# A gated cross-attention and expert layer: the row of score maxima is split by row group, and the next batch's queries move from units 0 to 3 to units 4 to 7

## What is computed

```python
# x (16,100,128), ctx (16,1444,96)
q = ln(x) @ w_q;  k = ctx @ w_k;  v = ctx @ w_v            # 16 heads of 64
attn = softmax(q @ k.T / 8)                                # 100 x 1444 per head
x = x + tanh(g_xattn) * ((attn @ v) @ w_o + b_o)
x = x + tanh(g_ffn) * ffn(ln(x))    # self-attention, 16 heads of 8, then top 2 of 8 experts + shared
```

## Time and profile before

| what | us |
|---|---|
| median of 3 runs (range) | 1325.35 (1325.32 to 1327.8) |
| the profiled execution's own time | 1323.73 |
| its span, first to last instruction | 1322.0 |
| TensorE busy | 1249.3 (95%) |
| VectorE busy | 935.8 (71%) |
| ScalarE busy | 824.1 (62%) |
| GpSimd busy | 767.5 (58%) |
| granted TensorE clock, mean | 0.984 of full speed |

### The profile page before, as it was taken

How to read it: one execution, slowest core, us unless ns; L and a number is a source line. 1 busy time by engine, 2 the same in 40 slices (tenths; PEclk the granted TensorE clock), 3 DMA queues, 4 the chain that set the end, 5 groups by cost and what they waited for, 6 DMA issues and landing times.

```text
span 1322.0 us, 34615 instructions
## 1 busy us (share of the span) xinstructions
PE 1249.3 (95%) x14472; PEld 911.7 (69%) x14472; DVE 935.8 (71%) x1714; ACT 824.1 (62%) x1476; POOL 767.5 (58%) x603
## 2 busy tenths in 40 slices
PE   6789999999999999999999999999999999789998
PEld 5356777777677777777776767677777776567776
DVE  5697776768675868685858676767767685956676
ACT  1345666667666766666666666666666666555654
POOL 3144666565656566665656565756565646654554
PEclk9798999999999999999999999999999999999999
DMA  6201503030313030302020302111021300000000
GB/s 172 65 1 34 167 14 80 14 80 14 81 13 81 13 80 14 80 10 77 13 74 15 78 16 55 40 41 53 18 75 14 63 14 15 14 15 1 8 8 14
DMA packets 122278, 57.28 MB, mean 43 GB/s; under 512 B 108262, under 2 KB 117706, under 8 KB 122122
## 3 DMA queue, kind: packets, MB, share of 16 engines
q1 hardware_dynamic: 122122, 55.07, 17.5%
HBM read 15.38 MB, written 0.82 MB: 12 GB/s over the span
## 4 chain that ended last, share of the span: by engine, by line
PE 73%; DVE 13%; ACT 10%; issue 3%; DMA 1%; SPq 0%; DVEq 0%; ACTq 0%
PE psum L777 17%; PE psum L758 9%; PE psum L858 8%; PE psum L759 8%; PE psum L760 8%; PE psum L793 5%; PE psum L890 3%; PE psum L912 3%; PE psum L903 3%; PE psum L805 3%; DVE mx L1309 3%; DVE p_lo L449 2%; DVE kbd L1329 2%; ACT p L985 2%; ACT p_hi L991 2%
## 5 line engine op out<-in xcount | busy, mean ns | idle before, releaser
L449 POOL TENSOR_TENSOR p_lo<-p,p_hi 128x768 f16<-128x768 f32 (+1 forms) x192 | 349.6, 1827 | 256.0 <-ACT p_hi L986 163.3
L1309 DVE TENSOR_REDUCE mx<-psum 128x1 f32<-128x512 f32 (+1 forms) x585 | 360.8, 651 | 38.5 <-PE psum L858 32.9
L985 ACT ACTIVATE p<-psum 128x768 f32<-128x768 f32 (+1 forms) x256 | 215.0, 840 | 243.6 <-PE psum L760 243.4
L777 PEld LDWEIGHTS psum<-c_both,p_hi 128*128 128x128 f16 x4992 | 255.2, 98 | 61.7 <-issue 30.3
L777 PE MATMUL psum<-c_both,p_hi 128*128 128x97 f16 (+1 forms) x4992 | 281.2, 207 | 2.1 <-ACT acc_sb L1001 1.1
L758 PE MATMUL psum<-qk_hi,cT_both 97*128 97x384 f16 (+1 forms) x768 | 259.6, 338 | 17.2 <-ACT p_hi L991 9.1
L759 PE MATMUL psum<-qk_lo,cT_both 96*128 96x384 f16 (+1 forms) x768 | 258.4, 336 | 0.0
L760 PE MATMUL psum<-qk_hi,cT_both 96*128 96x384 f16 (+1 forms) x768 | 256.3, 334 | 0.0
L858 PE MATMUL psum<-cT_both,qk_hi 96*128 96x512 f16 (+1 forms) x585 | 215.9, 369 | 10.9 <-DVE kbd L1329 4.9
L449 DVE TENSOR_TENSOR p_lo<-p,p_hi 128x768 f16<-128x768 f32 (+1 forms) x192 | 205.0, 1068 | 16.7 <-ACT p_hi L986 15.3
L990 ACT ACTIVATE p<-psum 128x384 f32<-128x384 f32 (+1 forms) x256 | 130.0, 508 | 135.5 <-PE psum L760 135.5
(11 more groups left out here) (201 smaller groups left out, 2115.7 us busy)
## 6 DMA issues: line engine op xcount, KB each, us to landing
c_both<-c_new SPq DMA_DIRECT2D x16, 768.0 KB, 3.5
ctx_nat<-in_ctx_dram SPq DMA_DIRECT2D x16, 528.0 KB
aT<-a_new SPq DMA_TRANSPOSE x64, 2.9
wg<-in_L_ffn_e_gate_dram SPq DMA_DIRECT2D x1, 1024.0 KB, 5.5
wu<-in_L_ffn_e_up_dram SPq DMA_DIRECT2D x1, 1024.0 KB, 7.8
wd<-in_L_ffn_e_down_dram SPq DMA_DIRECT2D x8, 128.0 KB, 4.9
out_dram<-x SPq DMA_DIRECT2D x4, 200.0 KB
x<-in_x_dram SPq DMA_DIRECT2D x1, 600.0 KB
```

Of the source, the lines that this page charges most:

```text
L449: engine.tensor_tensor(p_lo[0:m, i % 3, 0:w], p32[0:m, i % 3, 0:w], p_hi[0:m, i % 3, 0:w], ALU.subtract).then_inc(lo_made(b, i)[0], 1)
L777: t = mm(psum[:, ACCB + bank, k * (C + 1):k * (C + 1) + wide], p[0:m, i % 3, n * P:(n + 1) * P], c[parity][0:m, j, 0:wide], start=(j == 0 ...
L985: a(to32, src, ACT.Exp, scale=DH ** -0.5)
L1309: v.tensor_reduce(mx[:, rt, part:part + 1], bank[:, 0:w], AX.X, ALU.max)\
```

## The change

The maxima are split by row group. Those of the first (tiles 0 to 5, 18 of the 39) and of two more tiles (`AHEAD`, 24) are still found a batch ahead, now in units 10 to 23 of the batch before; the other 15 (tiles 8 to 12) are found as units "o" in units 0 to 9 of the batch itself. Each group gets its own transposition (m in unit 21, m1 in unit 10), its own `mrow` and its own DMAs: `send_second_row` sends tiles 6 to 11 and the short tile 12, and unit 12 (`i == CH`) waits for them. The next batch's queries are made in units 4 to 7. Ahead of batch 0 only 8 tiles are reduced, and m stands behind the sixth. In batch 0 the layer-norm units move to units 0 to 10, and ScalarE's conversion of batch 1's context goes from unit 0 to unit 3. The last batch now has the 15 o units and m1. The diff, cut to its core:

```diff
-    for n, i in enumerate((0, 1, 2, 3)):
+    for n, i in enumerate((4, 5, 6, 7)):
         plan[i].append(("q", n))
...
-    share = {i: 0 for i in range(3, 21)}
-    for n in range(NPU):
-        i = min(share, key=lambda i: (load[i], i))
...
+    NP0 = TILES[0] * MP
+    AHEAD = NP0 + 2 * MP
...
+    for i, n in spread(range(AHEAD, NPU), range(10)):
+        plan[i].append(("o", n))
+    for i, n in spread(range(NP0), range(10, 21)) + spread(range(NP0, AHEAD), range(21, UNITS)):
+        plan[i].append(("p", n))
+    plan[10].append(("m1", 0))
+    plan[21].insert(0, ("m", 0))
...
+    LN_UNITS = ((0, 1, 3, 4), (3, 4, 6, 7), (6, 7, 9, 10))
+    RSTD_UNITS = (2, 5, 8)
     for n in range(1, 4):
-        plan[2 * n + 5].append(("la", n))
-        plan[2 * n + 6].append(("lb", n))
-        plan[2 * n + 8].append(("lc", n))
-        plan[2 * n + 9].append(("x", n))
+        for kind, i in zip(("la", "lb", "lc", "x"), LN_UNITS[n - 1]):
+            plan[i].append((kind, n))
...
-    PREP = [("q", 0), ("q", 1)] + [("w", n) for n in range(3)] + [("q", 2)] + \
-           [("w", n) for n in range(3, 6)] + [("q", 3)] + [("w", n) for n in range(6, RT)] + [("m", 0)]
+    PREP = [("q", 0), ("q", 1)] + [("w", n) for n in range(3)] + [("q", 2)] + [("w", n) for n in range(3, 6)] + \
+           [("m", 0), ("q", 3)] + [("w", n) for n in range(6, AHEAD // MP)]
...
-        mrow = sb("mrow", [RT, P], F16)
+        mrow = [sb(f"mrow{r}", [TILES[r], P], F16) for r in range(2)]
...
             def send_row(b, parity, free):
 
                 sp.wait_ge(aux_free, free + 1)
-                sp.dma_start(qk_hi[parity][C:C + 1, 0:(RT - 1) * P], mrow[0:RT - 1, :]).then_inc(row_in, 16)
+                sp.dma_start(qk_hi[parity][C:C + 1, 0:ROW0[1]], mrow[0][:, :]).then_inc(row_in, 16)
+
+            def send_second_row(b, parity, free):
+
+                sp.wait_ge(aux_free, free + 1)
+                sp.dma_start(qk_hi[parity][C:C + 1, ROW0[1]:(RT - 1) * P], mrow[1][0:TILES[1] - 1, :]).then_inc(row2_in, 16)
                 sp.dma_start(qk_hi[parity][C:C + 1, (RT - 1) * P:ROWS],
-                             mrow[RT - 1:RT, 0:rows_of(RT - 1)]).then_inc(row_in, 16)
+                             mrow[1][TILES[1] - 1:TILES[1], 0:rows_of(RT - 1)]).then_inc(row2_in, 16)
...
                     ctx_made(b + 1, 1 - parity)
                     turn(b - 1, 1)
+                    second_row_of(b, kind, parity)
...
                 if i == 0:
-                    pe.wait_ge(row_in, (b + 1) * 32)
+                    pe.wait_ge(row_in, (b + 1) * 16)
+                    if isinstance(b, int) and b == 0:
+                        pe.wait_ge(wide_free, AHEAD // MP)
+                if i == CH:
+                    pe.wait_ge(row2_in, (b + 1) * 32)
...
-                    if kind == "first" and i == 0:
+                    if kind == "first" and i == 3:
                         ctx_hi_parts(1, kind, 1)
...
-                    if n == NPU - 1:
+                    if n in (NP0 - 1, NPU - 1):
+                        r = int(n == NPU - 1)
+                        tiles = (slice(0, TILES[0]), slice(TILES[0], RT))[r]
                         dve.wait_ge(aux_free, free + 1)
-                        v.tensor_reduce(mx_row[:, :], mx[:, :, :], AX.X, ALU.max).then_inc(max_step, 1)
+                        v.tensor_reduce(mx_row[:, tiles], mx[:, tiles, :], AX.X, ALU.max).then_inc(max_step, 1)
...
-                    cp(mrow[:, :], bank[0:RT, 0:P // 2].bitcast(F16)).then_inc(aux_free, 1)
+                    cp(mrow[r][:, :], bank[0:TILES[r], 0:P // 2].bitcast(F16)).then_inc(aux_free, 1)
```

More of the change, by code:

```diff
@@ L85, in flamingo_kernel, with spread @@
         load[i] += 0 if i - 1 in LO_POOL else .9
-    share = {i: 0 for i in range(3, 21)}
-    for n in range(NPU):
-        i = min(share, key=lambda i: (load[i], i))
[L89 to L96, removed]
+    NP0 = TILES[0] * MP
+    AHEAD = NP0 + 2 * MP
+    def spread(maxima, units):
+        counts = {i: 0 for i in units}
+        for _ in maxima:
+            i = min(counts, key=lambda i: (load[i], i))
+            counts[i] += 1
+            load[i] += .6
+        left = iter(maxima)
+        return [(i, next(left)) for i in units for _ in range(counts[i])]
+    for i, n in spread(range(AHEAD, NPU), range(10)):
[4 more added lines that the diff above has]
+    plan[21].insert(0, ("m", 0))
     ROUTER = ["max", "sub", "sum", "inv", "prob", "best0", "tie0", "rank0", "first0", "pick0", "drop",
@@ L160, in one_maxima_first @@
     def one_maxima_first(units):
-        maxima = [u for u in units if u[0] == "p"]
+        maxima = [u for u in units if u[0] in ("p", "o")]
         if sum(u[0] not in NO_BANK for u in units) < 3 or not maxima:
@@ L169, in places_of @@
         banked = [u for u in units if u[0] not in NO_BANK]
-        early = bool(banked) and banked[0][0] == "p"
+        early = bool(banked) and banked[0][0] in ("p", "o")
         where = {0: [], 1: [3], 2: [1, 3], 3: [0, 1, 3] if early else [1, 2, 3], 4: [0, 1, 2, 3] if early else [1, 1, 2, 3],
@@ L210, in flamingo_kernel @@
     LN_A, LN_B = ["sum", "mean", "centred"], ["square", "sumsq", "lnvar"]
+    SET_NAMES = {"la": lambda n: [f"{k}{n}" for k in LN_A], "lb": lambda n: [f"{k}{n}" for k in LN_B],
+                 "lc": lambda n: [f"xln{n}"], "x": lambda n: [f"xhi{n}"], "nh": lambda n: [f"Nh{n}"],
+                 "x1": lambda n: [f"x1 {n}"]}
     SET_DVE = [f"{n}0" for n in LN_A + LN_B] + ["wqT", "xln0", "Mh0hi", "Mh0", "xhi0", "xlnT0", "tn", "bot", "Mh1lo"] + \
-              [f"{n}1" for n in LN_A + LN_B] + [f"{n}2" for n in LN_A] + ["xln1"] + [f"{n}2" for n in LN_B] + \
-              ["Nh0", "xhi1"] + [f"{n}3" for n in LN_A] + ["Nh1", "xln2"] + [f"{n}3" for n in LN_B] + \
-              ["Nh2", "xhi2", "x1 0", "Nh3", "xln3", "x1 1", "xhi3", "x1 2", "x1 3"]
+              [name for us in steps("first")[0] for place in us for k, n in place if k in SET_NAMES
+               for name in SET_NAMES[k](n)]
     SET_ACT = ["wkT", "tx", "tf", "Mh1", "wvT"]
@@ L528, in row_of, with second_row_of @@
                 send_row(b + 1, 1 - parity, aux_base(b, kind)[1] + steps(kind)[1][("m", 0)][1])
+            def second_row_of(b, kind, parity):
+                if kind != "first":
+                    sp.wait_ge(scores, b * UNITS)
+                send_second_row(b, parity, aux_base(b, kind)[1] + steps(kind)[1][("m1", 0)][1])
             ctx_made(0, 0)
+            send_row(0, 0, numbered(PREP)[("m", 0)][1])
             ctx_made(1, 1)
-            send_row(0, 0, AT_FIRST - 1)
+            second_row_of(0, "first", 0)
             turn(0, 0)
@@ L551, in _ @@
             turn(B - 2, 1)
+            second_row_of(B - 1, "last", 1)
             turn(B - 1, 0)
@@ L673, in body @@
                 for i in range(UNITS):
-                    if kind == "first" and i in (9, 11, 13):
-                        token_rstd((i - 7) // 2)
+                    if kind == "first" and i in RSTD_UNITS:
+                        token_rstd(RSTD_UNITS.index(i) + 1)
                     if i == CTX_LO_AT and b + 2 < B:
@@ L854, in aux @@
                         pe.wait_ge(ct_in, (b + 1) * 16)
-                    if part == 0 and rt % 3 == 0 and rt // 3 < 4:
+                    if kind == "p" and part == 0 and rt % 3 == 0:
                         pe.wait_ge(aux_free, out_of(("q", rt // 3)))
@@ L859, in aux @@
                            cT_hi[parity][0:C, part * MW:part * MW + w], start=True, stop=True)
-                elif kind == "m":
-                    pe.wait_ge(max_step, (b + 1) * 2)
-                    t = tr(bank[0:RT, 0:P // 2].bitcast(F16), mneg[:, :], ident16[:, :])
+                elif kind in ("m", "m1"):
+                    r = int(kind == "m1")
+                    tiles = (slice(0, TILES[0]), slice(TILES[0], RT))[r]
+                    pe.wait_ge(max_step, (2 * b + r + 1) * 2)
+                    t = tr(bank[0:TILES[r], 0:P // 2].bitcast(F16), mneg[:, tiles], ident16[:, :])
                 elif kind == "x":
@@ L1283, in aux @@
                     scores_of = psum[:, 3 * (n % 2):3 * (n % 2) + MP, :].rearrange("p b w -> p (b w)")[:, 0:KV]
-                    v.tensor_reduce(mx_row[:, n:n + 1], scores_of, AX.X, ALU.max).then_inc(wide_free, 1)
-                    if n == RT - 1:
-                        dve.wait_ge(wide_free, RT)
-                        ts(mneg[:, :], mx_row[:, :], -1.0, SHIFT, ALU.mult, ALU.add).then_inc(max_step, 2)
+                    if n == TILES[0]:
+                        set_wait(dve, set_pool, SET_POOL, "mx")
+                    into = mx_row[:, n:n + 1] if n < TILES[0] else mx[:, n, 0:1]
+                    v.tensor_reduce(into, scores_of, AX.X, ALU.max).then_inc(wide_free, 1)
+                    if n == TILES[0] - 1:
+                        dve.wait_ge(wide_free, TILES[0])
+                        ts(mneg[:, 0:TILES[0]], mx_row[:, 0:TILES[0]], -1.0, SHIFT, ALU.mult, ALU.add).then_inc(max_step, 2)
                     return
```

31 lines of the change are left out of this document (18 added, 13 removed).

## The result

The changed kernel takes 1404.98 us (median of 4 runs, 1403.3 to 1406.28), the kernel before 1325.34 beside it (4 runs, 1323.58 to 1327.8). The ratio is 1.0606, with a 95% interval of 1.0591 to 1.0622: 6% slower, where I had forecast half a per cent faster. The profiled span is 1403.8 us instead of 1322.0.

What follows compares the result with a forecast made beforehand. TensorE, busy for 95% of the span, was taken as the bound. Stretch ahead -9.4, batch 0 -4, middle batches +4.2 and last batch +3 sum to -6.2: 1325.35 - 6.2 = 1319 us, range 1305 to 1333.

Steps and rivals of the forecast that it cites:

- (a): Middle batch, units 4 to 7: queries ahead of probs_rest and a maximum on VectorE make TensorE wait; +1.25 us a batch.
- the ring of banks: Middle batch: three banks go round, so o37 waits 1.0 us for o35's bank, and q1 in unit 5 0.25 for q0's.
- the one on the slow side: The second row makes it slower: TensorE waits 1.8 us at unit 12, time 1335 us; chance 0.26.
- The rest of the middle batch: Middle batch: costs 1.25, 0.8 and 0.1 less gains of 1.85 give +0.3 us, times fourteen +4.2.
- The gains: Middle batch: of 2.3 us lost, 0.45 stays (0.2 in units 1 to 3, 0.25 in 22 and 23); -1.85 us.
- Unit 5: Middle batch, unit 5: its earlier loss of 0.4 us goes, and q1 waiting for q0's bank costs 0.25.
- (b): Unit 12: the second row, copied behind kbd and three reductions, lands late; TensorE waits 0.8 us in each batch.
- the estimate beside it: Unit 12: a fixed DMA cost of about 2.0 us from the Trainium skill makes the row's wait 1.1 us.
- The stretch ahead: Ahead of batch 0: five of thirteen tile reductions go, and unit 0 starts at about 41.7 instead of 51.08; -9.4 us.
- Batch 0: Batch 0: moved pieces fill VectorE's idle time; -1 us for units 0 to 16, -3 for 17 to 23, together -4.
- The last batch: Last batch: fifteen maxima and m1 come in, and VectorE has no room in units 8 to 12; +3 us.

Runs made afterwards that it cites:

- the added wait: Changed kernel plus one wait: GpSimd, before its low half of unit 7, waits until VectorE has made that of unit 6; 1335.84 us, ratio 1.0088.
- the kernel before made late: Kernel before the change, with VectorE's low half of unit 6 moved behind all of unit 7's other VectorE work; 1331.15 us, ratio 1.0052.

## Why the prediction was wrong

**The step that failed is (a)**, "VectorE's subtraction of 0.57 at 2.7, probs_rest of 0.94 at 3.5". The order in it was right and the ring of banks too. The 0.94 was not: it came from a place where VectorE's subtraction had begun ahead of GpSimd's next instruction (487.98 and 488.22 in the kernel before) and wasn't held, and I carried it to one where GpSimd was about to run for 3.2 us. It measured 4.38. I had asked what stands behind q3 on VectorE, and not what runs on GpSimd at the new time. With the hold taken away, unit 8 loses 1.08, against the 1.0 that I had worked out. The hold therefore makes 3.9 of unit 8's 4.97, and the half clock behind it most of unit 9's 1.57. Together they are the 5.5 by which the added wait shortened this middle batch (75.56 to 70.05); in the later batches it is 5.0. None of my rivals was this one; the one on the slow side had the second row as its place.

**The rest of the middle batch** without the hold came to 70.05, which is +1.0 where I had +0.3. The gains were right (units 0 to 3 lose 0.1 or less each, 22 and 23 lose 0.17, where I kept 0.45). Unit 5 was taken too low, and that is the 0.7: my sum had struck off its 0.4 of before and left 0.25 in it, and 0.92 was lost. Its low half of unit 3 is 1.97 long beside GpSimd's normalisation, so this is in part the same error in small; placed first, it gave back 0.28.

**(b) The second row**: 0.8 forecast, 0.82 measured in the changed kernel, 0.83 in another, and removed with 0.86. The landing time taken from the earlier trace rows held: from the end of the copy (536.36) to TensorE's next matmul (539.05) it is 2.69 again, so the wait was the 0.8 of my sum and not the 1.1 of the estimate beside it. The chain in the changed kernel, VectorE, SP and TensorE:

```profile
536.16 0.20 DVE L1358 COPY mrow<-psum 7x128 f16<-7x128 f16 x1
```

```profile
536.44 0.73 SPq L490 DMA_DIRECT2D qk_hi<-mrow  x1
537.21 0.57 SPq L491 DMA_DIRECT2D qk_hi<-mrow  x1
```

```profile
539.05 0.34 PE L789 MATMUL psum<-qk_hi,cT_both 97*128 97x416 f16 x1 [0.66 <-DMA qk_hi<-mrow]
```

That moving m1 would save it was open to me, since my step counted three reductions between kbd and the copy. I had written that the copy can't be earlier than kbd; it didn't have to be.

**The stretch ahead** gave 8.2, not 9.4. Unit 0 starts at 42.90 where I said 41.7. VectorE, and TensorE at the end:

```profile
38.85 0.57 DVE L1288 TENSOR_TENSOR qk_lo<-psum,qk_hi 96x400 f16<-96x400 f32 x1 [1.49 <-ACT qk_hi L995]
39.52 3.23 DVE L1320 TENSOR_REDUCE mx<-psum 128x1 f32<-128x1444 f32 x2
```

```profile
42.90 0.48 PE L789 MATMUL psum<-qk_hi,cT_both 97*128 97x384 f16 x1 [2.21 <-DVE mx L1320]
```

Tile 6's reduction starts at 39.5, and I had 38.4. Half of the 1.1 was there before m0: the sixth tile ended at 36.4, where I had 35.9. m0 and q3 behind it took 3.1 and not 2.5. Five reductions at 1.6 are as I had them.

**Batch 0** gave 2.7 (4 forecast, between ends of -15 and +4). **The last batch** took 4.6 more in units 0 to 23 and 3.9 with what follows (3 forecast); of it the held split is a part, worth 1.0 in the batch's length and 2.3 to the end when it was taken away.

Without the hold the change would still have been slower. In the kernel with the added wait the span is 12.0 over that of before: the stretch ahead gives 8.6, the way from unit 0 to batch 1's kbd gives 0.3 (107.4 for 107.7), the thirteen batches from that kbd to the one of batch 14 cost 14.5 (911.8 for 897.3), and what follows costs 6.3, the held split in it. So with the failed step mended the time is 1335.8, just outside the range; the errors left are unit 5, the stretch ahead, batch 0 and the last batch, all taken too well.

## What to carry to other kernels

Before an instruction of VectorE is moved, look at what GpSimd runs at its new time: a duration read at the old place need not hold at the new one. When a line's longest instance is several times its median (here 4.38 for 1.02, and 8.22 for 0.61), look at GpSimd's timeline for an unbroken run of instructions that ends just before it does; the cure is to let VectorE go first, or to make GpSimd wait, which gained 69 us. The copy of a transposed row that must be sent back belongs ahead of whatever can wait, here three reductions, but not earlier than its input is ready: one unit too early cost TensorE 1.5 a batch.

## What the runs showed of the hardware

In the two places of the changed kernel shown above a VectorE instruction did not get in between GpSimd instructions that followed each other without a gap: it was held over the rest of one and two more (4.38), and over the rest of one and four more (8.22), until GpSimd's queue had a pause. The rule of the Trainium skill (SBUF — State Buffer, SBUF: two separate sides), that the other blocks for the whole instruction, would give a wait of one GpSimd instruction, by my estimate 1.6 here from the pair's 3.24; these two places show several.

It isn't so everywhere. Later in the same middle batch of the changed kernel VectorE's subtraction waited for one instruction of GpSimd's only and got in ahead of the next, which had no gap before it (VectorE, then GpSimd):

```profile
549.51 1.46 DVE L460 TENSOR_TENSOR p_lo<-p,p_hi 128x832 f16<-128x832 f32 x1
```

```profile
548.42 1.66 POOL L645 TENSOR_TENSOR a_new<-acc_sb,acc_rc 128x576 f16<-128x576 f32 x1
550.05 1.92 POOL L646 TENSOR_TENSOR acc_sb<-acc_sb,acc_rc 128x576 f32<-128x576 f32 x1
```

In the kernel before it got in between hn and xf, and xf took 1.26 for 0.79. GpSimd's losses in the places shown are 0.47 (xf), 0.57 (the pair) and 0.71 (L646).

Start times alone don't tell who wins. VectorE's subtraction started 0.43 into xf in the changed kernel and was held; it started 0.44 into xf in the kernel with the added wait, 0.51 into xf in the kernel before made late, and 0.44 into hn in the kernel before, and was not. Between the first two only GpSimd's next instruction differs: it was free to go in the one and made to wait in the other. But it was free to go in the last two as well. What decides between one instruction and several stays open. In the kernel with the added wait xf is drawn 1.89 long for 0.79; whether it was held, or its end is drawn up to the wait, the traces don't settle.

After TensorE had stood still for 4 us it went on at half clock (0.59 granted in unit 9), and this cost another 1.5 us or so in each batch. So a stall that recurs is dearer than its length.
